# GpSimd issues the gather of an expert's rows two experts ahead instead of one

## The chip, the cores and the metric

The kernel runs on one core of one Trainium2 chip. The metric is the device time of one execution in microseconds; the median of three runs of the kernel before is 2577.28 us. The engines are named as in the profile: PE is TensorE's matmul side and PEld its weight loads, DVE is VectorE, ACT is ScalarE, POOL is GpSimd, and SP is the queue that issues plain DMAs.

## What is computed

The input x is 4 x 2048 x 256, that is 8192 tokens of 256 numbers. It goes through causal attention with four heads and rotary positions, a residual and a layer norm (call the result x1), then through a mixture of 32 experts, a residual and a last layer norm. The change touches the experts alone:

```python
cap = int(CAP_FACTOR * T / E)                      # 320 rows for each of 32 experts
score = jnp.where(routed, probs, -jnp.inf)
idx = jnp.argsort(-score, axis=0)[:cap].T          # each expert's tokens
valid = jnp.take_along_axis(routed.T, idx, 1)
w = jnp.take_along_axis(Wc.T, idx, 1) * valid
xe = xf[idx]                                       # the gather
gate, upv = jnp.split(jnp.einsum('eci,eji->ecj', xe, w_up), 2, axis=-1)
ye = jnp.einsum('ecj,eoj->eco', silu(gate) * upv, w_down)
out = jnp.zeros((T, C)).at[idx.reshape(-1)].add((w[..., None] * ye).reshape(-1, C))   # the scatter
```

Beside each expert a small shared adapter (inner width 128) is applied to the same rows and added in with a factor of 0.05.

## The kernel before

The kernel has four stages behind one another: attention, routing (which writes the token lists `slot_token` and weights `slot_weight` of all experts), `experts`, and `last_norm`. In the profiled execution the experts take from about 1897 to 2533 us.

In `experts` each engine has its own program, and semaphores tie them together. An expert's 320 rows are three slots of 128, 128 and 64 rows. Tiles that carry an expert's data exist twice and are used by the expert's parity r = e mod 2: `rows` (gathered rows), `out` (result rows), `token_in`, `token`, `weight`, `w` and `w_raw`.

- PE (lines 1442 to 1504) does for expert e: `up(e)`, 60 matmuls of 320 columns in five pairs; then `turn(e + 1)` (line 1446), six transposes of the next expert's gathered rows into `x_ps`, which waits for `gathered` of that expert; then `down(e)` (line 1478), 45 matmuls of 256 columns. Before the loop stands `turn(0)`.
- ACT (line 1510) applies the silu to each pair, copies the upper parts of the next expert's weights (line 1512) and of h (line 1538), then the upper part of the transposed rows (line 1516), and at last scales the three result slots into `out` (line 1547). The first of these waits for `staged`, since it reads `weight`.
- DVE (line 1553) makes h (line 1578), the lower parts of the weights (line 1559), of h (line 1583) and of the transposed rows (line 1564).
- SP (line 1384) loads the raw weights of expert n as soon as the split of expert n - 2 is done (line 1388).
- POOL (line 1392) is a strict sequence for each expert: `gather(e + 1)` (a copy of the token list, line 1404, then three indirect DMAs, line 1407), `stage(e)` (two small copies, lines 1418 and 1419) and `scatter(e)` (three indirect DMAs that add into `acc`, line 1427, each waiting for its slot of `out`).

A gather into `rows[:, r]` first waits until PE has transposed what the tile held: line 1402 waits for `xe_turned` to be e - 1 for the gather of expert e. The count is one for each finished turn, so e - 1 means that the turns of experts 0 to e - 2 are done.

`pairs_of_experts` (line 1366) unrolls the first two and the last two experts and loops over the others by pairs. In this text T is the time at which PE starts `up(e)`, and "T + 8.8" is 8.8 us later.

Of the kernel before, what the change touches and what calls it, by code (L numbers as in the profile page):

```python
# [13 lines left out]
E = 32  # L14
# [26 lines left out]
def wait(eng, semaphore, value, passed):  # L41


    eng.wait_ge(semaphore, value)
    if not isinstance(value, int):
        eng.sem_inc(passed, 1)
# [1274 lines left out]
def experts(nc, dram, T, cap, slot_token, slot_weight, w_raw, w_loaded):  # L1321
# [8 lines left out]
    with ExitStack() as ctx:  # L1330
# [35 lines left out]
        def pairs_of_experts(eng, body):  # L1366

            for r in range(2):
                body(r, r, first=True, last=False)
            with eng.Fori(1, E // 2 - 1) as i:  # L1370
                for r in range(2):
                    body(2 * i + r, r, first=False, last=False)
            for r in range(2):
                body(E - 2 + r, r, first=False, last=r == 1)

        def ring(e, r):

            return (e - r) // 2

        def lists(tensor, e):  # L1380
            return tensor[:, bass.ds(e, 1), :].rearrange("p a b -> p (a b)")

        @block.sync
        def _(sp):
            with sp.Fori(1, E // 2) as i:
                for r in range(2):

                    wait(sp, w_split, PAIRS * (2 * i + r - 1), sp_passed)
                    load_weights(sp, dram, w_raw, w_loaded, 2 * i + r, i, r)

        @block.gpsimd
        def _(pool):
            pool.memset(ident[:], 0.0).then_inc(cleared, 1)
            pool.memset(rows[:], 0.0).then_inc(cleared, 1)
            wait(pool, cleared, 2, pool_passed)
            pool.affine_select(out=ident[:], in_=ident[:], compare_op=ALU.not_equal, fill=1.0, base=0,
                               pattern=[[-1, P]], channel_multiplier=1).then_inc(ident_set, 1)

            def gather(e, r, free):
                if free:  # L1400

                    wait(pool, xe_turned, e - 1, pool_passed)
                    wait(pool, gathered[r], 16 * SL * ring(e, r), pool_passed)
                pool.tensor_copy(token_in[:, r, :], lists(slot_token, e)).then_inc(listed_in, 1)  # L1404
                wait(pool, listed_in, e + 1, pool_passed)
                for t, n in enumerate(slots):
                    pool.indirect_dma_start(  # L1407
                        out=rows[0:n, r, t, :], out_offset=None, in_=dram["x1"],
                        in_offset=bass.IndirectOffsetOnAxis(ap=token_in[0:n, r, t:t + 1], axis=0),
                        bounds_check=T - 1, oob_is_err=False).then_inc(gathered[r], 16)  # L1410

            def stage(e, r, free):

                if free:

                    wait(pool, scattered, 16 * SL * (e - 1), pool_passed)
                    wait(pool, out_ready, SL * (e - 1), pool_passed)
                pool.tensor_copy(token[:, r, :], lists(slot_token, e)).then_inc(staged, 1)
                pool.tensor_copy(weight[:, r, :], lists(slot_weight, e)).then_inc(staged, 1)

            def scatter(e, r):
                wait(pool, staged, 2 * e + 2, pool_passed)

                wait(pool, scattered, 16 * SL * e, pool_passed)
                for t, n in enumerate(slots):
                    wait(pool, out_ready, SL * e + t + 1, pool_passed)
                    pool.indirect_dma_start(  # L1427
                        out=dram["acc"], out_offset=bass.IndirectOffsetOnAxis(ap=token[0:n, r, t:t + 1], axis=0),
                        in_=out[0:n, r, t, :], in_offset=None, bounds_check=T - 1, oob_is_err=False,
                        compute_op=ALU.add).then_inc(scattered, 16)  # L1430

            def body(e, r, first, last):
                if not last:
                    gather(e + 1, 1 - r, not first or r == 1)
                stage(e, r, not first)
                scatter(e, r)

            gather(0, 0, False)
            pairs_of_experts(pool, body)
            wait(pool, scattered, 16 * SL * E, pool_passed)  # L1440

        @block.tensor
# [303 lines left out]
```

## Time and profile before

| | us |
|---|---|
| median of three runs | 2577.28 (2570.64 to 2580.52) |
| span of the profiled execution | 2586.7 |
| PE busy | 2069.4 (80%) |
| DVE busy | 1516.8 (59%) |
| ACT busy | 1338.2 (52%) |
| POOL busy | 793.3 (31%) |
| from the start of up(1) to the start of up(31) | 576.62 |

The profiled execution's own time is its span, 2586.7 us from its first to its last instruction. It is 9.4 us over the median of the runs without a profile. The busy times are of the whole program; for the experts' stage only a stretch of the timeline tells which engine sets the pace. In the timeline rows the columns are the start, the duration, the engine, line and operation, and in brackets how long the engine had been idle and what ended that.

### The profile page before, as it was taken

The page shows a single profiled execution, that of the slowest core. Times are in us where ns is not written, and L with a number is a line of the kernel's source. Part 1 is how long each engine was busy: PE and PEld are TensorE (multiplying, and loading weights), DVE is VectorE, ACT ScalarE, POOL GpSimd, SP SyncE. Part 2 cuts the span into 40 slices and gives each one's busy share as a digit, 9 for nine tenths or more (in the row PEclk, how much of TensorE's full clock was granted, in tenths as well). Part 3 has the DMA queues.
Part 4 walks back from the last instruction along what each step waited for, and adds up shares of the span by engine and source line. Part 5 has one row for each costly group of instructions (what it writes and reads, how often), then busy time and mean ns, then how long its engine had stood idle before and what let it go on. Part 6 is the DMA issues. An engine that isn't in the chain of part 4 may idle for free. (4 is left out here: it accounts for less than half of the span.)

```text
span 2586.7 us, 45555 instructions
## 1 busy us (share of the span) xinstructions
PE 2069.4 (80%) x14340; PEld 1866.9 (72%) x14340; DVE 1516.8 (59%) x3366; ACT 1338.2 (52%) x3381; POOL 793.3 (31%) x889
## 2 busy tenths in 40 slices
PE   6899997899997799997899985311568888888880
PEld 5799886798886698886798874301457887888880
DVE  6555666555665455666556663688745455454444
ACT  5566664566664566664466543000455455555545
POOL 1122241222331122242101111000755555555543
PEclk9899998899997799997899976555889899999995
DMA  1000001000010000001000002000023333444327
GB/s 57 13 18 18 26 27 32 17 18 18 26 32 28 19 18 18 26 26 31 13 14 20 20 25 82 0 0 0 0 75 109 120 112 117 133 119 128 110 48 260
DMA packets 79907, 127.51 MB, mean 49 GB/s; under 512 B 15652, under 2 KB 69904, under 8 KB 75628
## 3 DMA queue, kind: packets, MB, share of 16 engines
q1 hardware_dynamic: 63852, 114.99, 12.8%
q0 software_dynamic: 15872, 10.24, 2.7%
q8 instruction: 95, 1.56, 0.3%
q14 instruction: 88, 0.72, 0.1%
HBM read 100.29 MB, written 35.65 MB: 53 GB/s over the span
## 5 line engine op out<-in xcount | busy, mean ns | idle before, releaser
L458 PE MATMUL out_ps<-v_sb,probs_t 128*128 128x64 f32 x4352 | 559.5, 274 | 46.1 <-DVE probs_t L749 35.7
L458 PEld LDWEIGHTS out_ps<-v_sb,probs_t 128*128 128x128 f32 x4352 | 540.5, 196 | 55.8 <-DVE probs_t L749 52.8
L735 DVE TENSOR_REDUCE part_max<-scores_ps 128x1 f32<-128x512 f32 (+3 forms) x576 | 357.3, 622 | 299.0 <-PE scores_ps L426 233.9
L426 PE MATMUL scores_ps<-k_st,q_parts 128*128 128x512 f32 (+3 forms) x1280 | 418.9, 411 | 23.5 <-POOL q_parts L863 14.2
L605 ACT ACTIVATE probs<-scores_ps,neg_max 128x512 f32<-128x512 f32 (+3 forms) x640 | 397.4, 626 | 61.0 <-DVE neg_max L739 46.7
L614 ACT COPY probs_t<-probs_t_ps 128x512 f32<-128x512 f32 (+3 forms) x416 | 208.7, 502 | 282.6 <-PE probs_t_ps L443 281.5
L443 PE MATMUL probs_t_ps<-ident,probs 128*128 128x128 f32 x2176 | 352.7, 278 | 2.3 <-DVE probs_t L749 2.2
L443 PEld LDWEIGHTS probs_t_ps<-ident,probs 128*128 128x128 f32 x2176 | 265.3, 144 | 54.4 <-issue 6.4
L1457 PE MATMUL up_ps<-xe_t,w 128*128 128x320 f32 x1920 | 289.1, 310 | 2.3 <-DVE xe_t L1564 1.7
L1457 PEld LDWEIGHTS up_ps<-xe_t,w 128*128 128x128 f32 x1920 | 283.8, 189 | 2.9 <-issue 1.9
L426 PEld LDWEIGHTS scores_ps<-k_st,q_parts 128*128 128x128 f32 x1280 | 207.6, 200 | 37.0 <-issue 16.3
L885 POOL TENSOR_TENSOR rstd<-mean_var,power 128x1 f32<-128x1 f32 x64 | 37.8, 591 | 622.2 <-DVE mean_var L791 622.2
L1427 POOL DMA_INDIRECT acc_rows<-out_rows,token x96 | 148.3, 1545 | 244.5 <-ACT out_rows L1547 233.3
L1578 DVE SCALAR_TENSOR_TENSOR h<-silu,up_ps 128x320 f32<-128x320 f32 x160 | 77.2, 482 | 234.4 <-ACT silu L1534 234.4
L1457 PE MATMUL y_ps<-w,h_parts 128*128 128x256 f32 x1440 | 210.3, 314 | 0.0
L1457 PEld LDWEIGHTS y_ps<-w,h_parts 128*128 128x128 f32 x1440 | 203.7, 221 | 2.5
L906 POOL TENSOR_TENSOR products<-qk,cos_sin 128x256 f32<-128x256 f32 x144 | 102.7, 746 | 228.3 <-ACT qk L543 228.3
L1559 DVE TENSOR_TENSOR w<-w_raw,w 128x768 fp32r<-128x768 f32 x160 | 153.1, 959 | 5.0 <-ACT w L1512 1.0
L749 DVE COPY probs_t<-probs_t_ps 128x512 f32<-128x512 f32 (+1 forms) x224 | 145.8, 651 | 1.5 <-PE probs_t_ps L443 0.8
L1407 POOL DMA_INDIRECT rows<-x_rows,token_in x96 | 129.2, 1346 | 49.3 <-POOL token_in L1404 29.6
L1512 ACT CAST w<-w_raw 128x768 fp32r<-128x768 f32 x160 | 131.8, 826 | 2.0 <-PEq L936 2.0
L1077 ACT ACTIVATE lane_off<-iota_p,lane_at 128x128 f32<-128x128 f32 x64 | 24.9, 390 | 206.0 <-POOL lane_at L1045 206.0
(219 smaller groups left out, 3229.8 us busy)
## 6 DMA issues: line engine op xcount, KB each, us to landing
w_raw<-in_w_expert SPq DMA_DIRECT2D x32, 1536.0 KB, 6.4
w_raw<-in_w_adapter SPq DMA_DIRECT2D x32, 384.0 KB, 6.8
x_t<-in_x_t SPq DMA_DIRECT2D x64, 128.0 KB, 2.1
x_row<-in_x SPq DMA_DIRECT2D x64, 128.0 KB, 2.0
x_rows<-x SPq DMA_DIRECT2D x64, 128.0 KB, 1.7
acc_rows<-x SPq DMA_DIRECT2D x64, 128.0 KB, 1.8
ln_x<-acc_rows SPq DMA_DIRECT2D x16, 512.0 KB, 6.2
out_rows_dram<-ln_y SPq DMA_DIRECT2D x16, 512.0 KB, 5.2
```

The lines of the kernel that those rows point to most:

```text
L426: mm = pe.matmul(out, q_parts[:, s % 2, part_, h, :], k_st[:, h, lo:hi], start=part_ == 0, stop=part_ == 1 and not diagonal)
L443: mm = pe.transpose(t_ps[:, g % 2, a - lo:a - lo + P], probs[:, g % PROBS_RING, a - lo:a - lo + P], ident[:])
L458: mm = pe.matmul(o_ps[:, h, :], probs_t[:, g % PT_RING, a - lo:a - lo + P], v_sb[:, a // P, h, :], start=a == 0, stop=a == t * P)
L605: act.activation(probs[:, g % PROBS_RING, 0:hi - lo], s_ps[:, bank[g], 0:hi - lo], ACT.Exp, bias=neg_max[:, u % 8:u % 8 + 1], accum_out=su ...
L614: act.copy(probs_t[:, g % PT_RING, 0:hi - lo], t_ps[:, g % 2, 0:hi - lo]).then_inc(probs_copied[1], 1)
L735: red = dve.tensor_reduce(neg_max[:, ring:ring + 1] if single else part_max[:, ring, c:c + 1], s_ps[:, bank[g], 0:hi - lo], AX.X, ALU.max, ...
L749: dve.tensor_copy(probs_t[:, g % PT_RING, 0:hi - lo], t_ps[:, g % 2, 0:hi - lo])\
L1407: pool.indirect_dma_start(out=rows[0:n, r, t, :], out_offset=None, in_=dram["x1"], in_offset=bass.IndirectOffsetOnAxis(ap=token_in[0:n, r, ...
L1427: pool.indirect_dma_start(out=dram["acc"], out_offset=bass.IndirectOffsetOnAxis(ap=token[0:n, r, t:t + 1], axis=0), in_=out[0:n, r, t, :], ...
L1457: mm = pe.matmul(o, left(a), right(b), start=start and n == 0, stop=stop and n == 2)
L1512: act.copy(columns(w[:, r, 0], p), columns(w_raw[:, r], p)).then_inc(w_upper, 1)
L1559: dve.tensor_tensor(columns(w[:, r, 1], p), columns(w_raw[:, r], p), columns(raw(w[:, r, 0]), p), ALU.subtract).then_inc(w_split, 1)
```

## The change

```diff
-            def body(e, r, first, last):
-                if not last:
-                    gather(e + 1, 1 - r, not first or r == 1)
+            def body(e, r, first, ahead):
+                if ahead:
+                    gather(e + 2, r, True)
                 stage(e, r, not first)
                 scatter(e, r)
 
-            gather(0, 0, False)
-            pairs_of_experts(pool, body)
+            for r in range(2):
+                gather(r, r, False)
+            for r in range(2):
+                body(r, r, first=True, ahead=True)
+            with pool.Fori(1, E // 2 - 1) as i:
+                for r in range(2):
+                    body(2 * i + r, r, first=False, ahead=True)
+            for r in range(2):
+                body(E - 2 + r, r, first=False, ahead=False)
             wait(pool, scattered, 16 * SL * E, pool_passed)
```

POOL's program alone changes. Two gathers stand before the first body. Body e then issues the gather of expert e + 2, into the tile of its own parity, where it issued that of expert e + 1 into the other. The helpers `gather`, `stage` and `scatter` stay as they are, and so do the tiles and all other engines. There are 32 gathers, 32 stagings and 32 scatters as before. The last two bodies have no gather; before, only the last had none.

## Rows read from the trace of the kernel before

**Rows 1.** Busy time of each engine from up(1) to up(31); columns in the first line
```profile
core 0: us, PE busy (x) PEld busy (x) DVE busy (x) ACT busy (x) POOL busy (x), PEclk, DMA share, GB/s
1933.22:2509.84 576.62, 499.59 (x3333) 476.19 (x3331) 288.61 (x480) 303.59 (x570) 317.03 (x271) 0.93 0.37 113
```

**Rows 2.** Groups of instructions in that stretch: busy, mean ns, idle before, releaser
```profile
L1452 PE MATMUL x_ps<-ident,rows 128*128 128x128 f32 x180 | 38.7, 306 | 77.0 <-DMA rows<-x_rows,token_in 77.0
```

**Rows 3.** Timeline of PE: turn(1), down(0) and up(1)
```profile
1926.64 1.16 PE L1452 MATMUL x_ps<-ident,rows 128*128 128x128 f32 x6
1927.73 5.65 PE L1457 MATMUL y_ps<-w,h_parts 128*128 128x256 f32 x45
1933.22 8.96 PE L1457 MATMUL up_ps<-xe_t,w 128*128 128x320 f32 x60
```

**Rows 4.** Timeline of PE inside the loop, and one turn late in it
```profile
2197.39 5.66 PE L1457 MATMUL y_ps<-w,h_parts 128*128 128x256 f32 x45
2202.89 8.96 PE L1457 MATMUL up_ps<-xe_t,w 128*128 128x320 f32 x60
2214.25 1.21 PE L1452 MATMUL x_ps<-ident,rows 128*128 128x128 f32 x6 [2.40 <-DMA rows<-x_rows,token_in]
2215.39 7.14 PE L1457 MATMUL y_ps<-w,h_parts 128*128 128x256 f32 x45
2222.36 8.96 PE L1457 MATMUL up_ps<-xe_t,w 128*128 128x320 f32 x60
...
2482.66 1.90 PE L1452 MATMUL x_ps<-ident,rows 128*128 128x128 f32 x6 [2.88 <-DMA rows<-x_rows,token_in]
```

**Rows 5.** Short stretches through the wait, the turn and the down of [rows 4]
```profile
2211.80:2214.20 2.40, 0.05 (x1) 0.00 (x0) 2.40 (x5) 1.62 (x4) 2.40 (x3) 1.00 0.17 44
...
2216.40:2217.40 1.00, 1.00 (x7) 1.00 (x6) 0.65 (x1) 0.00 (x0) 0.00 (x0) 0.50 0.95 393
...
2220.40:2221.40 1.00, 1.00 (x10) 1.00 (x9) 0.00 (x0) 0.47 (x1) 0.16 (x1) 1.00 0.30 120
```

**Rows 6.** Timeline of PE: up(31) and down(31), with no turn between them
```profile
2509.84 8.96 PE L1457 MATMUL up_ps<-xe_t,w 128*128 128x320 f32 x60
2518.64 5.73 PE L1457 MATMUL y_ps<-w,h_parts 128*128 128x256 f32 x45
```

**Rows 7.** Timeline of POOL for that expert: first scatter to last staging copy
```profile
2201.76 1.63 POOL L1427 DMA_INDIRECT acc_rows<-out_rows,token  x1 [5.74 <-ACT out_rows L1547]
...
2206.50 1.00 POOL L1404 COPY token_in<-slot_token 128x3 int32 x1
...
2211.74 1.36 POOL L1407 DMA_INDIRECT rows<-x_rows,token_in  x1 [0.30 <-issue]
...
2214.03 0.45 POOL L1419 COPY weight<-slot_weight 128x3 f32 x1
```

**Rows 8.** Timeline of ACT and DVE for that expert
```profile
2200.36 0.47 ACT L1547 ACTIVATE out_rows<-y_ps,weight 128x256 f32<-128x256 f32 x1 [2.17 <-PE y_ps L1457]
...
2213.08 0.96 DVE L1559 TENSOR_TENSOR w<-w_raw,w 128x768 fp32r<-128x768 f32 x1
...
2213.11 0.46 ACT L1538 CAST h_parts<-h 128x320 fp32r<-128x320 f32 x1
2213.95 0.48 DVE L1583 TENSOR_TENSOR h_parts<-h,h_parts 128x320 fp32r<-128x320 f32 x1
```

**Rows 9.** The gather's line: ns min/median/max of an issue, and time to landing
```profile
L1407 POOL DMA_INDIRECT rows<-x_rows,token_in x96: 943/1354/1894, 1901.2 to 2500.7; - x96
...
DMA to landing us min/median/max: 2.4/2.8/6.7
```

**Rows 10.** Timeline of POOL before up(0): an issue with DVE idle, the last staging copy
```profile
1904.66 0.96 POOL L1407 DMA_INDIRECT rows<-x_rows,token_in  x1 [0.30 <-issue]
...
1910.33 0.18 POOL L1419 COPY weight<-slot_weight 128x3 f32<-128x3 f32 x1
```

**Rows 11.** The weights: landing time of an issue, and SP's wait before it
```profile
w_raw<-in_w_adapter SPq DMA_DIRECT2D x32, 384.0 KB, 6.8
...
SPq L46 <- DVE w L1559: 527.8, 30, 25.1
```

## The prediction

> **What bounds the kernel now.** I read the busy times of the experts' stage first, then what its engines waited for, then one expert instruction by instruction. Between the starts of up(1) and up(31) PE is busy 499.6 of 576.6 us, and DVE, ACT and POOL only 289 to 317 us [rows 1]. So PE sets the pace, and what counts is the 77.0 us in which it is not busy. The groups of that stretch put all 77.0 on one place: the 30 turns (180 transposes) that wait for the gathered rows [rows 2]. The timeline shows it: up(e) starts at 2202.89, the turn at 2214.25 after 2.40 us of idling, and its releaser is the gather's DMA [rows 4]. Waits of other engines (POOL for ACT's result rows, ACT for PE) are those of engines with room and count for nothing.
>
> Why the gather is late: POOL finishes the scatters of expert e - 1 only after up(e) has begun, copies the list at 2206.50, issues the last of three gathers at 2211.74 until 2213.10 [rows 7], and a gather lands 2.8 us after its issue [rows 9]. PE would have been ready at T + 8.80, which is 2211.69; I take the 8.80 from the one expert with no turn behind its up, where down follows up by 2518.64 - 2509.84 [rows 6].
>
> The wait has a second price, the clock. In the idle stretch the granted clock still reads 1.00, but some 2 us later, in the middle of down, it is 0.50 (1.2 GHz), and at the end of down 1.00 again (2.4 GHz) [rows 5]. That down takes 7.14 us where one with no such dip takes 5.66 [rows 4]. Of the 30 downs of the stretch 19 are lengthened in this way, most by 1.5 us, and in three the turn also takes 1.90 in place of 1.21 us (one of them is among [rows 4]). The mean clock of the stretch is 0.93 [rows 1].
>
> **The change, part by part.** It removes and adds no work: 32 gathers, stagings and scatters stay. It moves each gather one expert earlier relative to its use.
>
> Its gain has a natural sample in the kernel before. Gather(1) is issued well ahead, and turn(1) starts with no wait: turn to down 1927.73 - 1926.64 = 1.09 us, down to up 1933.22 - 1927.73 = 5.49 us, with full clock in down [rows 3]. Together with the 8.80 of up [rows 6] an expert with its rows at hand takes 8.80 + 1.10 + 5.49 = 15.39 us (I round the turn up by 0.01 for the loop's 1.14 after a wait). Now an expert takes 576.62 / 30 = 19.22 us. The difference is 3.83 us, and it splits up: 77.0 / 30 = 2.57 us of visible wait, 0.16 us by which the modelled end of up (8.96) stands over 8.80, and 1.10 us of slower clock. Over the 30 experts 1 to 30 it is 576.6 - 461.7 = 114.9 us.
>
> Where the other turns stand: turn(0) waits for gather(0), whose place on POOL doesn't change, and turn(1) waits for nothing. Gain 0 for both. Expert 31 and the last norm are as before: 0.
>
> What each moved instruction is moved past. The new gather(e + 2) sits in POOL's queue where gather(e + 1) sat, behind the scatters of e - 1 and before staging(e). It issues one copy and three DMAs, as did the one that it replaces. So POOL's order per expert and the time of each instruction after T are unchanged. Its wait on line 1402 is for count e + 1, the turns 0 to e; turn(e) ran before up(e) began, so in the steady state it costs 0. Behind it on POOL are staging(e), for which ACT's first result slot waits, and for that slot in turn PE's third slot of down. In body 0 it costs something: turn(0) ends near 1913.4, and copy to last staging copy take 2214.48 - 2206.50 = 7.98 us [rows 7], so staging(0) ends near 1921.4 instead of 1910.5 [rows 10]. It is wanted in down(0), which starts at 1927.73 [rows 3]. Covered by 6 us: 0.
>
> What is late next, once turn(e + 1) starts at T + 8.80 and down at T + 9.90, from rows taken against T = 2202.89:
> - The fifth part of h is ready at 2213.95 + 0.48, T + 11.54 [rows 8]. Down reaches it after 18 of its 45 matmuls, at T + 9.90 + 18 x 0.122 = T + 12.1. Covered by 0.55 us. Turn(1) and down(0) show the same alignment with no loss [rows 3].
> - Staging(e) ends at 2214.48, T + 11.59 [rows 7]. ACT's first result slot starts 2.97 us into a down with no dip (2200.36 - 2197.39 [rows 4, 8]), at T + 12.87. Covered by 1.28 us; before, by 3.8 to 5.6. This is the thinnest new cover on another engine's queue. If it went, each us beyond it would cost about 30 us in all.
> - POOL as a loop of its own: result slot to first scatter 2201.76 - 2200.36 = 1.40, scatter to last staging copy 12.72 [rows 7, 8]: 14.12 us, under 15.39.
> - Weights: SP issues after the split at 2213.08 + 0.96 [rows 8], T + 11.2, for expert e + 3, wanted one whole expert later; landing takes 6.8 us, and SP now waits 527.8 / 30 = 17.6 us before each issue [rows 11]. Covered by over 10 us. The scatters now run beside this load; they start 14.3 us after T where before it was about 17 at the earliest, while the load runs from T + 11.4 to T + 18.2. Nobody waits for their landing before the next expert's scatter, so I take 0 and keep up to 0.5 us an expert (15 us) for the range.
>
> Result against the profiled execution: 2586.7 - 114.9 = 2471.8 us. That execution was 9.4 us over the median; I take the same for the one after: 2462.4, so 2463 us.
>
> A word on the cover of 1.28 us. An issue of a gather takes 0.96 us while DVE is idle [rows 10] but 1.35 us in the loop, and at most 1.89 [rows 9]: something beside DVE's work slows POOL.
>
> The Trainium skill, SBUF — State Buffer, section "Who interferes with whom", says that GpSimd shares a port pair with DVE, and that a DVE instruction with two SBUF inputs contends with a GpSimd instruction that reads SBUF. The rows agree in sign. By that rule a denser DVE could delay POOL further; by the timeline DVE's and POOL's instructions keep their places after T, so the sum stays.
>
> **The rivals.**
> (A) The forecast: waits and dips go. 2463, with 2455 to 2474 for its own spread. For it: turn(1) and down(0). Against it: one sample only, and POOL had no gather in flight there.
> (B) The waits go but the clock still dips as often, because something else than the waits brings it down. Then 30 x 2.73 = 82 us are saved: 2495. Against it: up(1), which follows an expert with no wait, and the last down, with no wait before it either, show no dip [rows 3, 6].
> (C) POOL becomes the bound. If its three gather issues took 1.89 us each and its other steps were 0.1 us longer, staging would end 1.6 + 0.6 = 2.2 us later, 0.9 us past its cover; 27 us of the gain are lost: 2490. It decides from 1.28 us of delay.
> (D) The gather isn't in fact earlier, for instance because POOL gets to it later by as much: 2577. The order in POOL's queue speaks against it.
> (E) Slower: the wait before the gather holds POOL's queue. This would be so if the tile that it writes came free only with turn(e + 1), at T + 9.90: then staging ends at T + 9.90 + 7.98 = T + 17.9, ACT's first result slot starts there, and the next up 2202.89 - 2200.36 = 2.53 us after that: 20.4 us an expert against 19.22, for 29 bodies +35 us: 2612. It decides where the count waited for is the turn of the expert after the present one. The code names turn(e), which speaks against it.
>
> **How the numbers follow.** A 0.74, B 0.08, C 0.11, D 0.03, E 0.02; 0.02 for savings beyond A. A, and B with most of C, make the range 2453 to 2497. A measurement of this kernel can tell about 0.5% from no change, 13 us. A, B and C are all faster by more: 0.95. D is the same: 0.03. E is slower: 0.02.
>
> **What would show it.** Right: PE's turns have no idle time for the gather's DMA but the first; all downs near 5.65 us; clock 1.00 from up(1) on; starts of up 15.4 us apart. B shows as waits gone with downs of 7.1 us. C shows as ACT's result rows released by POOL's staging, and PE idle within down. E shows as POOL idle before line 1404, released by PE. The prediction is wrong above all if PE meets another wait inside turn or down that the wait for the gather now covers.

## The result and the profile after

The changed kernel takes 2466.94 us (median of 2462.81 to 2469.38), the kernel before 2578.52 us in the runs made beside it. The ratio is 0.9563, with a 95% interval of 0.9545 to 0.9580: faster by 4.4%, 111.6 us. The profiled execution's span is 2466.2 us.

The experts' stage of the kernel after, from the start of up(1) to the start of up(31), in the same view and with the same columns as [rows 1]:

```profile
1928.49:2389.89 461.40, 461.40 (x3333) 447.22 (x3332) 285.97 (x480) 300.69 (x570) 310.65 (x267) 1.00 0.46 142
```

The same work takes 461.40 in place of 576.62 us. PE is busy in all of it, with the same number of matmuls (3333), and the granted clock is 1.00 where it was 0.93. Its 499.6 busy us have become 461.4, although nothing was taken from it. Of these 38.2 us, 30 x 0.16 = 4.8 us are only the modelled end of up, which no longer stands free ahead of an idle stretch, and some 1.5 us the turns, which take 1.09 us to down's start in place of 1.14 after a wait. The rest, about 32 us, is the slower clock. DVE, ACT and POOL are busy nearly as long as before (1 to 2% less) in a shorter time.

The turns in the groups of that stretch, the view of [rows 2], sit idle for nothing:

```profile
L1459 PE MATMUL x_ps<-ident,rows 128*128 128x128 f32 x180 | 34.6, 281 | 0.0
```

PE's timeline, the view of [rows 4]:

```profile
2189.95 8.96 PE L1464 MATMUL up_ps<-xe_t,w 128*128 128x320 f32 x60
2198.75 1.15 PE L1459 MATMUL x_ps<-ident,rows 128*128 128x128 f32 x6
...
2199.84 5.65 PE L1464 MATMUL y_ps<-w,h_parts 128*128 128x256 f32 x45
2205.33 8.96 PE L1464 MATMUL up_ps<-xe_t,w 128*128 128x320 f32 x60
```

With T = 2189.95 the turn starts at T + 8.80, down at T + 9.89 and the next up at T + 15.38. All thirty experts look like this, to 0.01 us, and each of their downs takes 5.65 us.

The other engines in that expert, the views of [rows 7, 8] (token's staging copy is L1418):

```profile
2193.54 1.03 POOL L1404 COPY token_in<-slot_token 128x3 int32 x1
...
2198.80 1.35 POOL L1407 DMA_INDIRECT rows<-x_rows,token_in  x1 [0.30 <-issue]
...
2200.14 0.96 DVE L1566 TENSOR_TENSOR w<-w_raw,w 128x768 fp32r<-128x768 f32 x1
2200.16 0.97 POOL L1418 COPY token<-slot_token 128x3 int32 x1
...
2201.01 0.48 DVE L1590 TENSOR_TENSOR h_parts<-h,h_parts 128x320 fp32r<-128x320 f32 x1
2201.09 0.45 POOL L1419 COPY weight<-slot_weight 128x3 f32 x1
...
2202.81 0.47 ACT L1554 ACTIVATE out_rows<-y_ps,weight 128x256 f32<-128x256 f32 x1 [1.58 <-PE y_ps L1464]
...
2204.20 1.63 POOL L1427 DMA_INDIRECT acc_rows<-out_rows,token  x1 [2.66 <-ACT out_rows L1554]
```

The issue of the last gather begins just as the turn of the next expert starts (2198.80 against 2198.75), which no longer matters: these rows are for the expert after it. Staging ends at T + 11.59 and ACT's first result slot, released by PE, starts at T + 12.86.

### The profile page after: what moved, and what is told of

Its sections match the earlier page's. It is cut to its first block and busy times, and to the rows that moved or that the text cites. A ratio compares the mean times of both kernels' runs of the same rounds, so it can differ in the third digit from the quotient of the medians.

```text
span 2466.2 us, 45555 instructions
## 1 busy us (share of the span) xinstructions
PE 2029.4 (82%) x14340; PEld 1836.2 (74%) x14340; DVE 1514.7 (61%) x3366; ACT 1335.0 (54%) x3381; POOL 789.5 (32%) x889
## 5 line engine op out<-in xcount | busy, mean ns | idle before, releaser
L1464 PE MATMUL y_ps<-w,h_parts 128*128 128x256 f32 x1440 | 181.0, 285 | 0.0
L1464 PEld LDWEIGHTS y_ps<-w,h_parts 128*128 128x128 f32 x1440 | 174.4, 191 | 2.2
```

Of the source, the lines that this page charges most:

```text
L1464: mm = pe.matmul(o, left(a), right(b), start=start and n == 0, stop=stop and n == 2)
```

## The experiments

Theory 1: the wait for the gather cost its own length and, through the clock, some 40% as much again in down; without it PE alone sets the pace. The rivals: the slower clock has another cause (B), POOL becomes the bound (C), and the wait in front of the gather can hold POOL's queue (E).

**The kernel before, profiled once more.**

> The kernel before once more, for its profile. If the 9.4 us by which its first profiled execution stood over the median came from the execution and not from the profiling, another profiled execution falls elsewhere, within 2570 to 2590 us, and the difference lies before up(1) as much as in the experts. If profiling itself adds time, the span is near 2586 again. Both theories expect the turns to wait 2.4 to 3.0 us in all 30 experts; the count of lengthened downs should be near 19 of 30 but need not be the same.

Its span is 2579.3 us and its time 2581.08 us, 1.4 us over the median of the 13 other runs of the kernel before in that comparison (2579.72 us). Those range from 2577.5 to 2588.98 us, and the slowest of them has a span of 2587.2 us, like the 2586.7 us of the first profile. So profiling adds at most a small part of the 9.4 us; most of them belonged to that one execution. In the new one up(1) starts 3.4 us earlier (1929.87 against 1933.22), and the stretch to up(31) is 4.1 us shorter:

```profile
1929.87:2502.42 572.55, 496.06 (x3332) 473.59 (x3331) 288.57 (x480) 303.29 (x570) 316.92 (x271) 0.94 0.38 114
```

18 of its 30 downs are lengthened, and one turn takes 1.90 us where in the first profile three did. The waiting is the same, 76.5 us against 77.0 [rows 2]. What varies from execution to execution of the kernel before is how often the clock falls, and the time at which the experts begin.

**Keeping PE at work while it waits.** Three kernels add matmuls to the kernel before that leave the wait's end where it was:

```diff
                 up(e, r)
                 if not last:
+                    for _ in range(20):
+                        pe.matmul(x_ps[:, 0, 320:512], w[:, r, 0, 0:P], w[:, r, 0, P:P + 192], start=True, stop=True)
                     turn(e + 1, 1 - r)
```

> The kernel before, with 20 extra matmuls of 192 columns whose result nobody reads, issued by PE after up(e) and before it waits for the gathered rows of e + 1. They take about 20 x 0.09 = 1.8 us of the 2.57 us of waiting, so the turn should start as late as before. Theory 1 (the wait brings the clock down): the dips in down go, and with them their 30 x 1.1 = 33 us: 2545 us. Rival (the dips have another cause, such as the weights' transfer beside down): the dips stay, 2578 us.

> As the former with 8 extra matmuls, about 0.7 us, which leaves some 1.8 us of idling. Theory 1: between the two, 2545 to 2578 us, with fewer than 19 lengthened downs. Rival: 2578 us and 19 of 30.

> As warm8 and warm20 with 14 extra matmuls ahead of the turn, 1.6 us by the 0.115 us of one that after_warm20 gave; about 1.0 us of idling is left. Theory 1 with a smooth dependence: half of the dips, about 2563 us. If the clock holds as soon as the idle stretch is short enough: no dip, 2550 us. If only a full cover counts: as warm8, 2573 us.

PE's timeline of the kernel with 20 extra matmuls, which stand at line 1501:

```profile
2199.84 8.96 PE L1457 MATMUL up_ps<-xe_t,w 128*128 128x320 f32 x60
2208.65 2.38 PE L1501 MATMUL x_ps<-w 128*128 128x192 f32 x20
2211.70 1.21 PE L1452 MATMUL x_ps<-ident,rows 128*128 128x128 f32 x6 [0.68 <-DMA rows<-x_rows,token_in]
2212.85 5.66 PE L1457 MATMUL y_ps<-w,h_parts 128*128 128x256 f32 x45
```

The turn still starts at T + 11.86, as late as in the kernel before (T + 11.36 in [rows 4], T + 11.90 in the expert after it), and still because of the gather's DMA; but down is short. So it is in all 30 experts:

| kernel | idle before a turn, us | lengthened downs of 30 | up(1) to up(31), us | time, us | ratio to before (95%) |
|---|---|---|---|---|---|
| before, first profile | 2.4 to 3.0 | 19 | 576.62 | 2578.52 | 1 |
| before, second profile | 2.4 to 2.9 | 18 | 572.55 | 2581.08 (one run) | |
| 8 extra | 1.5 to 2.0 | 17 | 569.86 | 2573.1 | 0.9974 (0.9960 to 0.9988) |
| 14 extra | 0.8 to 1.4 | 7 | 555.08 | 2558.06 | 0.9916 (0.9899 to 0.9932) |
| 20 extra | 0.2 to 0.7 | 0 | 544.98 | 2550.52 | 0.9879 (0.9852 to 0.9905) |

The ratios are to the runs of the kernel before made beside each kernel, whose median was 2579.72 us for 8 and 20 extra matmuls and 2579.27 us for 14; the 2578.52 us in the first row is the median of the four runs of the result.

Adding 600 useless matmuls in the loop makes the kernel 1.2% faster, 29 us by the medians and 28 to 32 us in the stretch, where I had expected 33. The turns start no earlier: at T + 11.53 on average with the extra matmuls, and at T + 11.53 and T + 11.51 in the two profiles without. So the gain is the clock alone, and rival B falls. Its mean granted clock in the stretch is 1.00:

```profile
1927.89:2472.87 544.98, 534.58 (x3932) 515.25 (x3931) 288.52 (x480) 303.91 (x570) 316.88 (x271) 1.00 0.39 118
```

With it the gain of the change splits without a model. From 576.62 or 572.55 to 544.98 us is the clock, 32 or 28 us; from 544.98 to 461.40 us is the wait, 84 us: 30 x (11.53 - 8.80) = 82 us by which the turns start earlier, and about 1.5 us for the turns themselves. The smaller doses were less clear-cut than either form of the theory that I gave. Eight extra matmuls left the count of long downs nearly as it was and gained 0.3%. Fourteen left seven, between my "half" and "none": fewer than half, and a time (2558) between the two predicted. The less PE idles, the rarer the slower clock, but the length of the wait alone doesn't decide: in the first profile waits of 2.38 us stand before long downs and before short ones. What decides between them these runs leave open.

**The same extra matmuls after the change.**

> The kernel after the change with the same 20 extra matmuls ahead of each turn. If PE is now without slack, each expert grows by their 20 x 0.09 = 1.8 us: 2467 + 31 x 1.8 = 2523 us, and the same extra work that is free or a gain before the change costs 56 us after it. If another engine set the pace after the change, the time stays at 2467 us.

2533.05 us, 66.1 us over the changed kernel, for 31 turns 2.13 us each. One extra matmul costs 66.1 / (31 x 20) = 0.107 us by the medians; by the profiles an expert takes 528.20 / 30 = 17.61 in place of 15.38 us, 0.111 each. I had taken 0.09, so the size was off by a fifth; the direction holds. The same edit that gains 29 us before the change costs 66 us after it. PE has no slack left, and nothing else sets the pace.

**How much POOL can be delayed.** Three kernels put a memset of its own tile ahead of the staging copies of the changed kernel:

```diff
             def stage(e, r, free):
...
+                pool.memset(idle[:], 0.0)          # idle: 128 x 900, x 2700 or x 4500
                 pool.tensor_copy(token[:, r, :], lists(slot_token, e)).then_inc(staged, 1)
```

> The kernel after the change, with a memset of 128x900 on POOL ahead of each staging; the memset of 128x1536 at the start took 1.38 us, so this one about 0.8 us. The prediction gave staging a cover of 1.28 us: the time should stay at 2467 us. If the cover is thinner than 0.8 us, or POOL sets the pace, it grows by up to 30 x 0.8 = 24 us, to 2491 us.

> As the former with a memset of 128x2700, about 2.4 us. By the cover of 1.28 us each expert grows by 2.4 - 1.3 = 1.1 us or a little less: 2467 + 33 = 2500 us, perhaps more if the idle time that arises in down brings the clock down. If POOL had room beyond the cover: 2467 us. If it had none: 2467 + 72 = 2539 us.

> As stage_late3 with a memset of 128x4500, about 3.95 us. In stage_late3 the memset took 2.37 us, but the two staging copies behind it took 0.36 instead of 1.42 us, and staging ended at T + 12.81, just where ACT's first result slot starts: the cover of 1.28 us was used up to the last tenth. With 1.58 us more each expert should grow by 1.3 to 1.6 us: 2467 + 30 x 1.45 = 2510 us, and more if the idle time in down brings the clock down. If the cover was larger than counted, the time stays near 2467 us.

They took 2465.18, 2463.49 and 2507.18 us, ratios to before 0.9574 (0.9545 to 0.9603), 0.9558 (0.9531 to 0.9586) and 0.9723 (0.9707 to 0.9739). The first came out as expected, but it didn't test the cover: the staging copy of the token list behind its 0.87 us memset takes 0.19 in place of 0.97 us, and staging ends at T + 11.59 to T + 11.61 in the experts of the loop, as without a memset. The second was a miss: 2.37 us of memset should have cost 33 us and cost nothing. The timeline of its POOL and ACT tells why:

```profile
2200.91 2.37 POOL L1419 MEMSET idle<- 128x2700 f32 x1
...
2203.22 0.19 POOL L1420 COPY token<-slot_token 128x3 int32 x1
2203.35 0.17 POOL L1421 COPY weight<-slot_weight 128x3 f32 x1
2203.57 0.47 ACT L1556 ACTIVATE out_rows<-y_ps,weight 128x256 f32<-128x256 f32 x1 [1.57 <-POOL weight L1421]
```

The staging copies take 0.19 and 0.17 us here, where they took 0.97 and 0.45 us: the memset pushed them behind DVE's last instruction of the expert. Start of the first copy to end of the second is 0.30 in place of about 1.38 us, so the delay pays back 1.1 us of itself. Staging ends at 2203.52, T + 12.81 with T = 2206.09 - 15.38. ACT, whose releaser is now POOL, still starts its first slot at 2203.57, T + 12.86 as before. The cover that I had counted, 1.28 us, was used up just to its end.

The third memset passes that end, and the expected 2510 us came out as 2507:

```profile
2201.90 3.87 POOL L1419 MEMSET idle<- 128x4500 f32 x1
...
2206.04 0.84 ACT L1556 ACTIVATE out_rows<-y_ps,weight 128x256 f32<-128x256 f32 x2 [3.07 <-POOL weight L1421]
...
2206.57 2.05 PE L1466 MATMUL y_ps<-w,h_parts 128*128 128x256 f32 x15 [1.14 <-ACT out_rows L1556]
```

POOL's staging releases ACT, ACT's first slot releases PE's third slot of down, and PE idles 1.14 us. Here staging ends at T + 14.32, 1.45 us past the cover, and an expert takes 501.90 / 30 = 16.73 us, 1.35 us more. The difference of 0.1 us is a second small cover: without a delay ACT's first slot ends at T + 13.33, and PE wants it at T + 9.89 + 30 x 0.122 = T + 13.55. This is rival C made into a kernel: it sets in once staging ends later than its cover allows, at the place that the prediction named.

**The gather held up in POOL's queue.**

```diff
-                    wait(pool, xe_turned, e - 1, pool_passed)
+                    wait(pool, xe_turned, e, pool_passed)
```

> The slower rival as a kernel: the kernel after the change, but the gather of e + 2 waits for the turn of e + 1 and not of e. The prediction priced it at 20.4 us an expert and 2612 us. If the gather that is held up costs nothing because staging has room, the time stays at 2467 us.

2594.79 us, ratio to before 1.0071 (1.0048 to 1.0093): slower than the kernel before, by 16 us, where I had priced it at 35 us slower. The chain is the one that was named (waits, longest first in total; then one expert of the timeline):

```profile
POOL token_in L1404 <- PE x_ps L1459: 212.6, 29, 7.8
ACT out_rows L1554 <- POOL weight L1419: 142.5, 29, 5.2
...
PE y_ps L1464 <- ACT out_rows L1554: 86.4, 29, 3.3
```

```profile
2206.96 9.60 PE L1464 MATMUL up_ps<-xe_t,w 128*128 128x320 f32 x60
...
2216.40 1.15 PE L1459 MATMUL x_ps<-ident,rows 128*128 128x128 f32 x6
...
2217.91 0.88 POOL L1404 COPY token_in<-slot_token 128x3 int32 x1 [7.58 <-PE x_ps L1459]
...
2222.54 0.95 POOL L1407 DMA_INDIRECT rows<-x_rows,token_in  x1 [0.30 <-issue]
...
2223.63 0.18 POOL L1419 COPY weight<-slot_weight 128x3 f32 x1
...
2224.37 2.73 PE L1464 MATMUL y_ps<-w,h_parts 128*128 128x256 f32 x15 [3.04 <-ACT out_rows L1554]
```

From the list's copy to the last staging copy POOL now needs 2223.81 - 2217.91 = 5.90 us, not the 7.98 us of [rows 7] with which I had priced it. It runs while DVE is mostly through with its expert, and an issue takes 0.95 to 1.10 us in place of 1.28 to 1.39. Against that, up takes 9.60 instead of 8.96 us and the last 15 matmuls of down 2.73 us instead of 2.05, since PE idles 3 us in down and its clock falls (0.93 on average over the stretch, 1.00 in the changed kernel). The mean is 589.96 / 30 = 19.67 us an expert, where I had 20.4 and the kernel before has 19.22.

**Staging ahead of the gather.**

```diff
             def body(e, r, first, ahead):
+                stage(e, r, not first)
                 if ahead:
                     gather(e + 2, r, True)
-                stage(e, r, not first)
                 scatter(e, r)
```

> The kernel after the change with staging(e) ahead of gather(e + 2) on POOL. It gives staging 6 us more cover and issues the gather 1.5 us later, 10 us before its use. If nothing but PE's own work sets the pace after the change, the time stays at 2467 us. If the order in POOL's queue still costs something, this one is faster.

2459.18 us, ratio to before 0.9547 (0.9513 to 0.9581), which overlaps the changed kernel's 0.9545 to 0.9580. Its stretch from up(1) to up(31) is 461.60 us against 461.40. The median is 7.8 us lower, but by the profiles 7.2 us of that lie before up(1) (1921.33 against 1928.49), where the executions of every kernel differ. In the experts there is no difference: the order in which POOL does these two costs nothing here.

## Why the prediction was right

The forecast was 2463 us, inside 2453 to 2497; the measured time is 2466.94 us.

**The bound and the wait.** PE was the bound, and the turns' wait was all of its idle time. This is confirmed by the 499.6 of 576.6 us busy in [rows 1] against 461.40 of 461.40 us, and by the extra matmuls that cost 66 us after the change.

**15.39 us an expert.** It came from one sample with the gather well ahead (turn(1) and down(0)) and one up without a turn behind it. Measured: 15.38 us, thirty times. 461.7 us were predicted for the stretch and 461.40 measured. The rows of the kernel before held the state after the change complete; that there was only one sample did no harm, since POOL's work kept its place after T.

**The split.** I had put 82 us on the wait and 33 us on the clock. With 20 extra matmuls it is 84 and 28 to 32 us.

**The covers.** Staging's end at T + 11.59 and its use at T + 12.87 were found at T + 11.59 and T + 12.86. The delay runs show that this cover was real and finite: used up by the 2.37 us memset, broken by the 3.87 us one. The fifth part of h cost nothing: each of the thirty downs takes 5.65 us. The scatters that now run beside the weights' load kept their issue times, 1.62 or 1.63 us for the first, and the load's last part lands 7.0 us after its issue where it took 6.8; the 15 us that I had kept in the range for it were not needed.

**What was off.** The sum came out 4 us low, about 0.15%. I took the gain from the profiled execution, and then took off all of the 9.4 us by which that execution stood over the median. But 4.1 of those 9.4 us lay in the experts (576.62 against 572.55 us in the second profile): that execution had met the slower clock more often. The change removes them, so the sum counts them twice. Against the second profile the stretch gains 572.55 - 461.40 = 111.2 us, and the medians differ by 111.6 us, where I had 114.9. Another 3.4 us of the 9.4 lay before up(1).

The kernel after has no such excess: 2466.2 us in profile and 2466.94 as the median. So the 9.4 us that I took off its forecast span had no counterpart, and that span, forecast at 2471.8 us, came out 5.6 us lower, 4.7 us of it before up(1) (1928.49 against 1933.22). The change has no part in these 4.7 us: from up(0) to up(1) it is 18.13 us before and 18.14 after. Two errors against each other, 9.4 and 5.6 us, leave the 4 us; that they partly cancel is luck. Up(0) started anywhere from 1903.2 to 1915.1 us in the profiles of this study. This is noise that no reading of one trace removes; a second profile of the kernel before would have told the two terms apart.

**The rival prices.** C was priced at 2.2 us of added delay for 27 us lost. The delay runs show the mechanism at its place and the point from which it decides, but what fills POOL's time matters: a delay that moves POOL's later work out from beside DVE pays part of itself back. E was priced 19 us too high for the same reason (5.90 for 7.98 us), with the clock's fall taking back a part. The same 7.98 us went into staging(0), which I put at 1921.4: from its list's copy to its last staging copy it takes 1913.56 - 1908.69 = 4.87 us, since DVE has little to do there. It had 6 us to spare by my count, so nothing came of it.

## What to carry to other kernels

When an engine that sets the pace waits for a transfer issued by an engine with room, look for the one place in the trace where that transfer happens to be early, such as the first round before the loop: it shows the pace after the change, what the wait does to the clock included. Count the wait itself and what PE's idling does to the granted clock as separate terms (here 84 and some 30 us), and read the second one from downs with and without it. A prefetch issued from a full queue is cheap as long as it takes the old one's place; write down the cover of whatever is queued behind it (here 1.28 us), since that is what the next change will hit.

## What the runs showed of the hardware

A PE that idles for 2.4 to 3.0 us in each round of 19 us had its clock at 1.2 GHz in the following matmuls in 18 or 19 of 30 rounds, each time at a cost of 1.3 to 2.0 us, mostly 1.5, in a down of 5.65 us. In the first profile the granted clock reads 0.50 within each of the 19 long downs, and 1.00 all through each of the 11 short ones. With idle stretches of 1.5 to 2.0 us it was 17 of 30, with 0.8 to 1.4 us 7 of 30, with 0.2 to 0.7 us none. Matmuls whose result nobody reads shortened the kernel by 29 us. In the run with 3.87 us of memset PE idled 1.14 us in every down and the clock stayed at 1.00 in the 15 matmuls behind it; the down of 7.04 us there is idle time and not a slow clock.

An extra matmul of 192 columns took 0.107 to 0.111 us at full clock, one of 256 columns 5.49 / 45 = 0.122 us and one of 320 columns 8.80 / 60 = 0.147 us. 192 columns are 0.60 of 320 but take 0.73 to 0.76 of the time.

Beside DVE's work POOL's small copies take 2.6 to 5 times as long as without it, and its issues 1.4 times: the token list's staging copy 0.97 against 0.19 us, the weights' 0.45 against 0.17 us, a gather's issue 1.35 against 0.95 us. The Trainium skill, SBUF — State Buffer, section "Who interferes with whom", says that the two share a port pair and that a DVE instruction with two SBUF inputs contends with a GpSimd instruction that reads SBUF. These runs agree. In the changed kernel the token list's staging copy runs in 30 experts beside DVE's `w<-w_raw,w`, which has both inputs in SBUF, and ends 0.03 or 0.04 us after it (2201.13 and 2201.10 in the rows above); the weights' copy ends 0.05 us after `h_parts<-h,h_parts` in the same rows. With staging ahead of the gather, the copy of `token_in` runs in 29 experts beside `h<-silu,up_ps`, which has one input in PSUM, and takes only 0.17 to 0.28 us. The memset of 128x900, which reads nothing, takes 0.87 us beside `w<-w_raw,w` and isn't held until its end. This is read from the order of the instructions; no kernel here changed DVE's work, and the gather's longer issues were not traced to one instruction.
